# Graph block on one Trainium2 core: five edits of the closing stage's order (tile 2 behind all units, first down product ahead of the totals, last outputs from PSUM)

## What is computed

```python
edge_index = jnp.stack([src, dst])
xn = _layernorm(x, axis=-1)
x = x + _L0_gnn_ref(xn, edge_index, ...) + _L0_mix_ref(xn[None], ...)[0]
x = x + _L0_ffn_ref(_layernorm(x, axis=-1)[None], ...)[0]

# graph part, end:            out = agg + node_features; layernorm(out) * ln_g + ln_b
# mix part, end:              layernorm(y + x1) * ln2_g + ln2_b
# feed-forward, on x3 = layernorm(x):
weights = einsum('bsd,do->bso', x3, wr) + br        # one gate per node
idx = top_k(weights, s // 2)                        # the last one dropped
h = gelu(x3[sel] @ w1 + b1)                         # 256 -> 1024
y = (h @ w2 + b2) * weights[sel]                    # 1024 -> 256
out = x + x3 + y (only where selected)
```

## Time and profile before

| | us |
|---|---|
| median of 3 runs | 1021.67 (1021.13 to 1023.03) |
| the profiled execution's own time | 1017.71 |
| its span | 1016.0 |
| TensorE matmul busy | 857.2 (84%) |
| VectorE busy | 781.5 (77%) |
| ScalarE busy | 608.5 (60%) |
| GpSimd busy | 601.6 (59%) |

### The profile page before, as it was taken

One profiled execution on the slowest core, in us unless ns is written; L12 is line 12 of the kernel. 1 busy time (PEld: TensorE's weight loads), 2 busy tenths in 40 slices (PEclk: granted clock), 3 DMA queues, 4 the chain that ended last, 5 costly groups with the idle time before them and its releaser, 6 DMA issues.

```text
span 1016.0 us, 18432 instructions
## 1 busy us (share of the span) xinstructions
PE 857.2 (84%) x5153; PEld 632.6 (62%) x5153; DVE 781.5 (77%) x1682; ACT 608.5 (60%) x1540; POOL 601.6 (59%) x745
## 2 busy tenths in 40 slices
PE   4999999994787878778777888878769679999998
PEld 3776777762444555555555555555449667888886
DVE  6855666662789999999999999999968648997441
ACT  2565667662586798888888888897632122332121
POOL 4704777776777777777777777776720436662000
PEclk9999999997597899999999888897879988999999
DMA  9822666666888888888888888887716723320020
GB/s 282 272 86 103 232 217 221 213 220 214 260 260 261 256 266 262 273 267 270 266 269 266 264 265 272 266 264 234 229 58 197 245 59 104 95 68 0 2 99 28
DMA packets 126204, 202.76 MB, mean 200 GB/s; under 512 B 19755, under 2 KB 94846, under 8 KB 126102
## 3 DMA queue, kind: packets, MB, share of 16 engines
q0 software_dynamic: 38992, 129.87, 40.2%
q1 hardware_dynamic: 76630, 61.86, 20.2%
q10 hardware_dynamic: 10480, 9.83, 3.0%
HBM read 160.50 MB, written 40.99 MB: 198 GB/s over the span
## 4 chain that ended last, share of the span: by engine, by line
PE 38%; POOL 20%; DVE 13%; issue 11%; ACT 7%; DMA 7%; SPq 2%; DVEq 0%; ACTq 0%; POOLq 0%
POOL big L1414 15%; PE ps L2431 5%; PE ps L931 5%; PE ps L1631 4%; PE ps L2418 4%; PE ps L2382 3%; DMA big<-kv_scratch,src_i 3%; PE ps L972 3%; DVE big L1836 3%; PE ps L943 2%; PE ps L919 2%; PE ps L1614 2%; POOL big L2280 2%; ACT edge L1491 2%; POOL big L2270 2%
## 5 line engine op out<-in xcount | busy, mean ns | idle before, releaser
L1414 POOL DMA_INDIRECT big<-kv_scratch,src_i x392 | 372.1, 949 | 122.6 <-issue 116.7
L1614 PE MATMUL ps<-edge 64*128 64x256 f32 x784 | 126.8, 446 | 55.8 <-DVE big L1779 23.8
L1631 PE MATMUL ps<-big,edge 128*64 128x256 f32 x784 | 132.6, 469 | 36.3 <-DVE big L1836 36.3
L1614 PEld LDWEIGHTS ps<-edge 64*128 64x128 f32 x784 | 79.4, 210 | 95.6 <-issue 58.4
L1779 DVE TENSOR_TENSOR big<-big,ps 128x1024 f32<-128x1024 f32 x98 | 119.2, 1216 | 12.0 <-DMA big<-kv_scratch,src_i 9.5
L1786 DVE TENSOR_REDUCE ps<-big 128x32 f32<-128x1024 f32 x98 | 120.1, 1225 | 2.5
L1836 DVE TENSOR_TENSOR big<-big,ps 128x1024 f32<-128x1024 f32 x98 | 118.0, 1205 | 0.0
L1491 ACT ACTIVATE edge<-edge 128x64 f32<-128x64 f32 x392 | 103.9, 339 | 1.6
L2344 ACT ACTIVATE big<-ps,fb 128x256 f32<-128x256 f32 (+2 forms) x104 | 39.5, 462 | 105.2 <-PE ps L2418 105.2
L1631 PEld LDWEIGHTS ps<-big,edge 128*64 128x64 f32 x784 | 56.1, 160 | 69.6 <-DVE big L1836 45.9
L2418 PE MATMUL ps<-big 128*128 128x256 f32 (+2 forms) x416 | 93.0, 381 | 2.8 <-ACT big L2331 2.8
(11 more groups left out here) (346 smaller groups left out, 1715.7 us busy)
## 6 DMA issues: line engine op xcount, KB each, us to landing
edge<-q_scratch SPq DMA_DIRECT2D x196, 64.0 KB
big<-kv_scratch,src_i POOLq DMA_INDIRECT x392
edge<-key_scratch SPq DMA_DIRECT2D x98, 64.0 KB
agg_scratch<-big SPq DMA_DIRECT2D x16, 252.0 KB
xn_scratch<-big ACTq DMA_DIRECT2D x5, 640.0 KB, 3.5
mix_scratch<-big SPq DMA_DIRECT2D x25, 128.0 KB, 1.8
mix_x_scratch<-big SPq DMA_DIRECT2D x25, 128.0 KB, 1.9
wmix<-mix_x_scratch ACTq DMA_DIRECT2D x25, 128.0 KB
```

The lines of the kernel that those rows point to most:

```text
L1414: pool.indirect_dma_start(kv_slots[s][:, k, :], None, kv_d[0:N, :], bass.IndirectOffsetOnAxis(ap=src_i[:, e:e + 1], axis=0)).then_inc(got[ ...
L1614: ins = pe.matmul(qr_ps[g % 2][:, (2 * hg + k) * D:(2 * hg + k + 1) * D], ohT[64 * hg:64 * hg + 64, g % 2, k * P:(k + 1) * P], qwin[64 * h ...
L1631: ins = pe.matmul(sums_of(g)[64 * hg:64 * hg + 64, :], oneh[:, g % OHRING, k, hg * 64:hg * 64 + 64], kv_slots[s][:, 2 * hg + k, D:2 * D], ...
```

## The change

1. `STATS_AT` and `X2_AT` become (13, 14): tile 2 no longer stands between the scales of units 15 and 16, but wholly in `first_three()`; x2 rows of tiles 2 and 3 are issued one unit earlier.
2. `LOADS` lists the loads: the four weight loads move from units 11 to 14 to units 0, 1, 3 and 4, the row parts behind them.
3. SyncE issues the x2 rows of tiles 4 and 5 behind `load_heads(1)`, ahead of its waits for the totals. GpSimd takes the second roots of tiles 0 and 1 before the first root of tile 2.
4. TensorE runs T1, D0, T2 before `all_totals()`; ScalarE copies tiles 1 and 2 before the totals. From slot 3 on at least five tiles are turned.
5. Tiles 16 to 24 (`kept` = 16) get the bias added to their rows ahead (`with_bias`), and `last_output` reads the down product from PSUM, in place of `keep_y` and `output`.

```diff
--- before.py
+++ after.py
@@ -72,8 +72,9 @@
 HW = max(H_OF)
 EARLY = 5
 EARLY_AT = HALF_AT + 3
-STATS_AT = (13, 14, 15)
-X2_AT = (14, 15)
+STATS_AT = (13, 14)
+X2_AT = (13, 14)
+LOADS = [("rows", 0), ("rows", 1), ("up", 0), ("up", 1), ("rows", 2), ("down", 0), ("down", 1)] + [("rows", i) for i in range(3, 13)]
 T_AT = 1
 W_AT = T_AT + NHG
 W_HALF = W_AT + H_OF[0] * WN
@@ -2091,6 +2092,7 @@
                 "xf", "row", "gate"))
             x3_T, x3_Tc, h_ps, hd, y_in, y_ok, out_ok, out_st = (sem(n) for n in (
                 "xf_turned", "xf_copied", "h_ps", "h", "y_ps", "y", "out", "out_stored"))
+            rb, out_last = sem("row_with_bias"), sem("out_from_ps")
             s_const3, s_cnt, s_tot, s_eq, s_eqsum, vsel = (sem(n) for n in (
                 "select_constants", "counted", "counts_summed", "equals_marked", "equals_summed", "select_step"))
 
@@ -2136,7 +2138,11 @@
 
             def turned(slot):
                 n = 1 + (TURNS[0] * (slot + 1) // TURNS[1] if slot >= NQ else 0)
+                if slot >= up_slot(1, 0):
+                    n = max(n, EARLY)
                 return min(NT, max(n, tiles_for.get(slot + 1, 0)))
+
+            kept = sum(1 for t in range(NT) if y_slot(t) < COUNT_AT + ROUNDS)
 
             def normed_before(t):
                 return GT - (-TURNS[0] * (y_slot(t) + 1) // TURNS[1])
@@ -2148,15 +2154,18 @@
                 sp.wait_ge(ue, NG)
 
                 def load_part(i):
-                    if i < len(MIX_PARTS):
-                        t, n = MIX_PARTS[i]
+                    if i >= len(LOADS):
+                        return
+                    kind, part = LOADS[i]
+                    if kind == "rows":
+                        t, n = MIX_PARTS[part]
                         sp.dma_start(rows[:, t:t + n, :], mix_d[t * P:(t + n) * P, :].rearrange("(t p) d -> p t d", p=P)
-                                     ).then_inc(mix_in[i % 3], 16)
-                    elif i < len(MIX_PARTS) + C:
-                        ch = i - len(MIX_PARTS)
+                                     ).then_inc(mix_in[part % 3], 16)
+                    elif kind == "up":
+                        ch = part
                         sp.dma_start(fw1[:, ch, :], a["L0_ffn_w1"][ch * P:(ch + 1) * P, :]).then_inc(s_fw, 16)
-                    elif i < len(MIX_PARTS) + C + 2:
-                        j = (i - len(MIX_PARTS) - C) * FS
+                    else:
+                        j = part * FS
                         sp.dma_start(fw2[:, j:j + FS, :], a["L0_ffn_w2"][j * P:(j + FS) * P, :].rearrange("(j p) d -> p j d", p=P)
                                      ).then_inc(s_fw, 16)
 
@@ -2216,6 +2225,8 @@
                 for i in range(2):
                     sp.wait_ge(ck_st[i], 16 * ((NU + 1 - i) // 2))
                 load_heads(1)
+                load_x2(4)
+                load_x2(5)
                 for t in range(EARLY):
                     sp.wait_ge(ga_in[t], 16)
                 for m in range(2):
@@ -2225,10 +2236,14 @@
                 for t in range(4, NT):
                     if t + 4 >= GR and t + 4 < NT:
                         load_xn(t + 4)
-                    load_x2(t)
+                    if t > 5:
+                        load_x2(t)
                 for t in range(NT):
                     n = P if t < NT - 1 else LAST
-                    sp.wait_ge(out_ok, t + 1)
+                    if t < kept:
+                        sp.wait_ge(out_ok, t + 1)
+                    else:
+                        sp.wait_ge(out_last, t + 1 - kept)
                     sp.dma_start(out[t * P:t * P + n, :], rows[0:n, t, :]).then_inc(out_st, 16)
                 sp.wait_ge(out_st, 16 * NT)
 
@@ -2287,12 +2302,12 @@
                     gather(t)
                 root(0, v3, mv3, rs3, r3)
                 root(1, v3, mv3, rs3, r3)
+                root(0, v4, mv4, rs4, r4)
+                root(1, v4, mv4, rs4, r4)
                 root(2, v3, mv3, rs3, r3)
-                root(0, v4, mv4, rs4, r4)
                 for i in range(2):
                     pool.wait_ge(ck_st[i], 16 * ((NU + 1 - i) // 2))
                 load_tails(1)
-                root(1, v4, mv4, rs4, r4)
                 root(2, v4, mv4, rs4, r4)
                 select_constants()
                 for t in range(3, NT, 2):
@@ -2347,13 +2362,12 @@
 
                 n = puts(0, 1)
                 for p in range(NPER + 1):
-                    if p == 1:
-                        n = puts(n, turned(y_slot(0)))
                     if p < NPER:
                         for q in range(NQ):
                             gelu(p, q)
                             n = puts(n, turned(up_slot(p, q)))
                     if p == 0:
+                        n = puts(n, turned(y_slot(0)))
                         keep_totals()
                     if p > 1:
                         for t in period(p - 1):
@@ -2422,7 +2436,8 @@
                 def down(t):
                     p, at = period_of(t), place(t) * P
                     pe.wait_ge(hd, (p + 1) * NQ)
-                    at_least(pe, y_ok, t - 1)
+                    at_least(pe, y_ok, min(t - 1, kept))
+                    at_least(pe, out_last, t - 1 - kept)
                     if t == 1:
                         pe.wait_ge(s_totalk[0], 2)
                         pe.wait_ge(s_totalk[1], 1)
@@ -2448,10 +2463,11 @@
                 pe.wait_ge(s_totalk[0], 1)
                 for p in range(NPER + 1):
                     if p == 1:
-                        all_totals()
+                        n = turns(n, 2)
                         pe.wait_ge(ck_kept, NCK)
                         down(0)
                         n = turns(n, turned(y_slot(0)))
+                        all_totals()
                     if p < NPER:
                         for q in range(NQ):
                             up(p, q)
@@ -2544,17 +2560,22 @@
                 def first_three():
                     with_rows(0)
                     ffn_stats(0)
+                    with_rows(1)
                     ffn_var(0)
-                    with_rows(1)
+                    ffn_stats(1)
+                    ffn_var(1)
+                    prepare_row(2)
                     normed(0)
-                    ffn_stats(1)
+                    with_mix_input(2)
+                    normed(1)
+                    gnn_stats(2)
+                    gnn_var(2)
+                    row_so_far(0)
+                    gate(0)
+                    gained(2)
                     with_rows(2)
-                    ffn_var(1)
                     ffn_stats(2)
                     ffn_var(2)
-                    row_so_far(0)
-                    gate(0)
-                    normed(1)
                     normed(2)
 
                 def normalise_pair(a):
@@ -2670,15 +2691,27 @@
                     dve.scalar_tensor_tensor(row, cols[:, :, t * P:(t + 1) * P], sel[:, t:t + 1], row, ALU.mult, ALU.add
                                              ).then_inc(out_ok, 1)
 
+                def with_bias(t):
+                    dve.scalar_tensor_tensor(rows[:, t, :], vecs["L0_ffn_b2"][:, :], sel[:, t:t + 1], rows[:, t, :], ALU.mult,
+                                             ALU.add).then_inc(rb, 1)
+
+                def last_output(t):
+                    dve.wait_ge(rb, t - kept + 1)
+                    dve.wait_ge(y_in, t + 1)
+                    dve.scalar_tensor_tensor(rows[:, t, :], ps[4 + t % 2][:, 0:D], sel[:, t:t + 1], rows[:, t, :], ALU.mult,
+                                             ALU.add).then_inc(out_last, 1)
+
                 dve.wait_ge(rwd, NT)
+                assert n == kept
                 m = 0
-                while m < NT:
-                    for t in range(m, min(m + 5, n)):
+                while m < kept or n < NT:
+                    if n < NT:
+                        with_bias(n)
+                        last_output(n)
+                        n += 1
+                    for t in range(m, min(m + 5, kept)):
                         output(t)
-                    m = min(m + 5, n)
-                    if n < NT:
-                        keep_y(n)
-                        n += 1
+                    m = min(m + 5, kept)
 
 _INS = ["x", "src", "dst", "edge_type_3", "node_type_6", "L0_gnn_Wk", "L0_gnn_Wq", "L0_gnn_bk",
         "L0_gnn_bv", "L0_gnn_Wv", "L0_gnn_relation_pri", "L0_gnn_Wm", "L0_gnn_ln_g", "L0_gnn_ln_b",
```

## The result

The median after is 1008.41 us (four runs, 1004.87 to 1013.3) against 1022.35 before (four runs): a ratio of 0.988, interval 0.985 to 0.991, so 9 to 15 us: a small change, under 2%, but clear of the noise. The profiled execution took 1004.87 us, span 1003.1, which is 12.9 under before's span.

What follows compares the result with a forecast made beforehand. Late-issued x2 rows make VectorE wait, and the end is tied to when it gets tile 5: 13.5 us earlier, 12.2 after TensorE's slow clock, plus 0.5 from last outputs, 12.7 off the 1021.67 median: 1009.0 us, range 1005.5 to 1015.

Steps and rivals of the forecast that it cites:

- Step 1, last unit: Around unit 16: tile 2's preparation leaves the place ahead, scale 8.2 us earlier, tile 0's first up products 8.0 us earlier.
- Step 1, weight loads: Early units: four weight loads moved to units 0, 1, 3 and 4 cost 0, with 4 us kept for the range.
- Rival D: Early units: weight loads hold them, up to 4 us off, gain 8.7 to 11, 1011 to 1013 us; chance 0.12.
- A: Whole kernel: the forecast itself, 12.7 us gained, own range 1007 to 1011 us; chance 0.55.
- Step 2: Totals to tile 5: down product first costs totals 1.8 us; gathers start at 824.0, VectorE starts tile 5 13.5 us earlier.
- Step 3: TensorE ahead of tile 5: waits 4.5 us, slow products cost 2.6 more; VectorE still decides, 12.2 us earlier.
- B: Ahead of tile 5: the clock holds through the 4.5 us wait; 14.0 us gained, 1007.7 us; chance 0.10.
- Step 4: Last outputs: reading PSUM directly leaves tile 24 one instruction, not two, saving 0.46 us.
- The sum: Whole kernel: 12.2 + 0.5 = 12.7 us gained, forecast 1009.0 us by the median.
- Rival C: Tile 0's products at half clock push totals and gathers by 4.6 us; gain 8.1, 1013.6 us; chance 0.18.
- E: Tile 0's products to tile 5: clock stays at half from 807 to 839, 4.6 us slower, 1026.3 us; chance 0.02.
- F: x2 rows: the wait only moves from tiles 2 and 4 to another tile, nothing gained, 1021 us; chance 0.03.

Runs made afterwards that it cites:

- three_behind_units: The changed kernel with the first half of tile 2 back behind unit 15's scale, its x2 rows still issued at unit 13; 1015.02 us.
- before_new_loads: The kernel before with only the weight loads moved to units 0, 1, 3 and 4; 1019.71 us.
- old_loads: The changed kernel with the weight loads back behind the row loads, at units 11 to 14; 1010.34 us.
- after_again: The changed kernel, unedited, run a second time; median 1009.21 us (six runs), ratio 0.988 to the kernel before.
- before_again: The kernel before, unedited, run a second time; 1016.64 us in one run.
- x2_late: The changed kernel with the x2 rows of tiles 4 and 5 issued behind the stored totals again; 1018.59 us in one run.
- totals_first: The changed kernel with the totals ahead of the first down product again; 1009.16 us.
- totals_rows_late: The changed kernel with totals ahead of the first down product and row loads of tiles 6 to 24 issued during the feed-forward; 1006.89 us in one run.
- totals_rows_spread: The changed kernel with totals ahead of the first down product, later row loads, and weight loads at units 0, 2, 4, 6; 1009.20 us, ratio 0.987.
- filler: The changed kernel with 16 useless products added on TensorE where it waits for tile 5; 1010.39 us.

## Why the prediction was right, point by point

The forecast of 1009.0 us met 1008.41, and its main path was the right one; but the nearness of the number is in part luck, as the sum below shows. By its own terms, counted from the first products so that the scatter of the edge loop is out:

**Step 1, last unit.** Right in effect: unit 15's products to tile 0's up products were to be 6.0 us (801.80 to 807.8) and were 5.55. Half wrong in its reason: it put 8.2 us on the place of tile 2. three_behind_units shows 2.0 us for the place; the rest is the wait for x2, which went with the earlier issue and the weights moved from ahead of it (before_new_loads, old_loads).

**Step 1, weight loads.** The mis-sized term. I took 0 and kept 4 for the range; a was 2.7 us longer in the profiled execution and 5.3 to 5.9 in after_again. The traffic of 755 to 783 came to 236 GB/s, near the 223 reckoned and under the 269 that was my reason for the 0, and still transfers came late. I had thought of ScalarE's waits for stores, and there was little of them; the loss is the wait of the early totals for their tails, which stand behind a store and land late themselves, and the half clock behind it: 1.56 and 1.5 us in the profiled execution. I also left out what the edit is good for: without it tile 0 waits 2.33 us for its weights (old_loads). Rival D, at 0.12, named the weights and the units but stores of ScalarE as the way, and was in part true beside A.

**Step 2.** Right nearly to the number. Gathers were to start 22.2 us behind unit 15's products (824.0 - 801.8) and started 22.10 behind them. Their landing, taken as 3.7, took 3.4. b was to shrink by 13.5 and shrank by 13.9 (13.2 between before_again and after_again). x2_late shows that 7.7 of it is the x2 rows of tiles 4 and 5. The cost of the down product ahead of the totals was said to be 1.8 us; the totals' start moved 2.0 in totals_first, where most of that is given back by the clock; in totals_rows_late, where it held, b is 1.6 shorter.

**Step 3.** Right in this execution, the clock included: a gap of 4.77 (4.5 forecast), products of 5.88 (6.2), the copy's wait 1.08 (1.3), and tile 21 turned 76.9 us behind the first use of tile 5 (76.4 forecast, 75.1 before). after_again lies between A and B: products of 4.75, no wait, 1.4 us less in c. The Trainium skill's remark (TensorE: Matmul & The Clock Gate, Part 1), that the point of change differs from run to run, agrees with 5.88 and 4.75 behind gaps of 4.77 and 4.47.

**Step 4.** 0.46 forecast, 0.39 measured. An output that reads its product from PSUM takes 0.48 us (998.70), as long as the one that read a copy, 0.48.

**The sum.** 12.7 forecast, 9.8 measured in the stage of the profiled executions (2.7 for the weights, and smaller ones), 8.5 between the means of two profiles each. The medians moved by 13.9 and, beside after_again, by 11.8. So the forecast took 3 to 4 us too much for the stage, and the medians moved 2 to 5 us more than the stage did. That is luck: in after's first profile the edge loop ended 3.0 us earlier and the weights cost 2.7, and the two cancel in the places that the prediction named (815.92 for totals at 816.3, 903.88 for 904). Where the rest of the medians' gain comes from is left open. The second interval (8 to 17 us) holds the stage's gain and the forecast alike, the first (9 to 15) holds 9.8 but not 8.5.

Rival C did not occur: tile 0's products ran in 3.81 us in every kernel with the x2 rows at unit 13, and in 5.53 to 5.78 in the two profiles of before (5.25 in before_new_loads). E did not occur: in after the clock fell behind one gap only between tile 0's products and tile 5. F did not either; with the x2 rows issued as in the change, a wait for them was left only where the weights stayed late (old_loads, 1.16).

## What to carry to other kernels

Ask of each wait when its transfer was issued and what was ahead of it in the queue: two small loads issued earlier were worth more here (7.7 us of b) than any reordering of engine work that was taken back alone, and large loads moved into a stretch with room on average can still go along with a late small transfer that something waits for. A wait of two to five microseconds on TensorE can be paid twice, once in itself and once in the clock behind it; forecast the second as a range from nothing to the full price. Where single runs scatter by more than the change, divide the stage at fixed rows and compare the pieces, and profile the unchanged kernel a second time before reading 1 us.

## What the runs showed that was not expected

TensorE went to half clock behind waits of 2.85 us (totals_first, pairs at 1.06 us) and 2.84 us (totals_rows_spread) and did not behind 2.86 us in totals_rows_late, whose totals start 12.4 us behind unit 15's products as well; early in the stage it fell behind 1.56 us and not behind 1.63. Sixteen products of no use in a wait of 4.8 us kept the clock at 1.00 and cost nothing (filler). And a gap of 4.5 to 5.1 us cost the products behind it anything from 1.1 to 2.3 us, not in the order of the gaps.
